# Layer 0's attention scores: one block-diagonal product over 128 rows, or four 32-row tiles of the TensorE array

## The reference

```python
q = hidden_state @ Wq + bq                      # 4096 x 1024 by 1024 x 1024
k = encoder_hidden_state @ Wk + bk              # 256 x 1024 by 1024 x 256
v = encoder_hidden_state @ Wv + bv
scores = jnp.einsum('bkgld,bksd->bkgls', q, k) * scale     # d = 32, s = 64
scores = scores + encoder_attention_mask[:, :, None, :, :]
attn = jax.nn.softmax(scores, axis=-1)
out = jnp.einsum('bkgls,bksd->bkgld', attn, v)
out = out.transpose(0, 3, 1, 2, 4).reshape(b, l, H) @ Wo + bo
x = out + hidden_state                          # then a layer norm
```

## Time and profile before

| | before |
|---|---|
| median of 3 runs | 1936.01 us (1934.52 to 1938.28) |
| the profiled execution, its own time | 1932.28 us |
| its span in the trace | 1930.5 us |
| PE busy, share of the span | 1826.7 us, 95% |
| DVE busy | 1082.6 us, 56% |
| POOL busy | 1032.3 us, 53% |
| ACT busy | 585.9 us, 30% |
| matmuls | 8640 |

### The profile page before, as it was taken

How to read it: one execution, slowest core, us unless ns; L and a number is a source line. 1 busy time by engine, 2 the same in 40 slices (tenths; PEclk the granted TensorE clock), 3 DMA queues, 4 the chain that set the end, 5 groups by cost and what they waited for, 6 DMA issues and landing times.

```text
span 1930.5 us, 22356 instructions
## 1 busy us (share of the span) xinstructions
PE 1826.7 (95%) x8640; PEld 1509.4 (78%) x8640; DVE 1082.6 (56%) x1086; ACT 585.9 (30%) x680; POOL 1032.3 (53%) x580
## 2 busy tenths in 40 slices
PE   5999999999988899999999977999999999999998
PEld 5788888888876777888778856887788778877887
DVE  6888888888867444444344456335633563356342
ACT  3444444444434332233332323112211221122111
POOL 2677777777758755465544656225522552255221
PEclk9999999999999999999999989999999999999999
DMA  8423333233163475655756554422342234132110
GB/s 204 108 76 82 83 79 78 74 81 85 45 191 111 131 235 201 198 180 175 242 188 211 189 189 153 152 77 83 136 153 66 100 118 153 66 118 101 66 55 33
DMA packets 249961, 244.43 MB, mean 127 GB/s; under 512 B 61440, under 2 KB 204928, under 8 KB 249856
## 3 DMA queue, kind: packets, MB, share of 16 engines
q1 hardware_dynamic: 248704, 241.97, 39.9%
q10 hardware_dynamic: 1152, 1.05, 0.2%
HBM read 157.99 MB, written 84.93 MB: 126 GB/s over the span
## 4 chain that ended last, share of the span: by engine, by line
PE 56%; DVE 19%; issue 9%; ACT 6%; POOL 4%; DMA 3%; SPq 2%; ACTq 0%; DVEq 0%; POOLq 0%
PE ps L53 18%; PE ps L55 18%; PE ps L54 18%; DVE small L972 4%; DVE pr L995 3%; ACT pr L741 3%; DVE pT1r L1006 2%; DVE pT0r L1006 2%; PE ps L648 2%; ACT ot L735 2%; DVE xT0r L902 1%; DVE xT1r L902 1%; POOL prob L1280 1%; DVE x2r L1075 1%; DMA xb<-in_x_dram 1%
## 5 line engine op out<-in xcount | busy, mean ns | idle before, releaser
L1275 POOL TENSOR_TENSOR prob<-prob,small 128x1024 f32<-128x1024 f32 x32 | 61.0, 1908 | 397.0 <-DVE small L1086 397.0
L1206 POOL TENSOR_TENSOR pr<-pr,small 128x1024 f32<-128x1024 f32 x64 | 122.0, 1906 | 100.0 <-DVE small L1001 100.0
L1082 DVE SCALAR_TENSOR_TENSOR prob<-ps,bias 128x1024 f32<-128x1024 f32 x32 | 39.1, 1222 | 227.6 <-PE ps L55 227.6
L840 ACT CAST x2Th<-x2r 128x1024 fp32r<-128x1024 f32 x32 | 33.6, 1050 | 424.6 <-DVE x2r L1075 424.6
L1227 POOL TENSOR_TENSOR xb<-xb,bo 128x1024 f32<-128x1024 f32 x32 | 79.9, 2497 | 141.0 <-DMA xb<-in_x_dram 141.0
L1201 POOL TENSOR_TENSOR pr<-pr,small 128x1024 f32<-128x1024 f32 x64 | 124.0, 1938 | 34.8 <-DVE small L976 34.6
L1050 DVE TENSOR_TENSOR y<-ps,xb 128x512 f32<-128x512 f32 x64 | 44.0, 687 | 159.3 <-PE ps L55 156.4
L972 DVE TENSOR_REDUCE small<-pr 128x16 f32<-128x1024 f32 x64 | 78.1, 1220 | 91.0 <-ACT pr L741 91.0
L53 PE MATMUL ps<-wo0h,oc0l 128*128 128x512 f32 x256 | 101.6, 397 | 0.0
L53 PE MATMUL ps<-wo0h,oc1l 128*128 128x512 f32 x256 | 101.0, 395 | 0.0
L53 PE MATMUL ps<-xT0h,wq0l 128*128 128x512 f32 x256 | 100.7, 393 | 0.0
(11 more groups left out here) (320 smaller groups left out, 5583.1 us busy)
## 6 DMA issues: line engine op xcount, KB each, us to landing
o_scratch<-ot SPq DMA_DIRECT2D x256, 64.0 KB, 1.8
ocr<-o_scratch SPq DMA_DIRECT2D x16, 1024.0 KB, 6.2
xb<-in_x_dram SPq DMA_DIRECT2D x32, 512.0 KB, 6.0
x_scratch<-y SPq DMA_DIRECT2D x32, 512.0 KB, 3.5
a_scratch<-ost SPq DMA_DIRECT2D x64, 256.0 KB, 3.0
b_scratch<-ost SPq DMA_DIRECT2D x64, 256.0 KB, 2.5
xd<-x_scratch SPq DMA_DIRECT2D x128, 128.0 KB, 2.8
raw<-b_scratch SPq DMA_DIRECT2D x32, 512.0 KB, 8.0
```

Source lines behind the costliest of these rows:

```text
L1206: nc.gpsimd.tensor_tensor(heads(v), heads(v), mx.unsqueeze(2).to_broadcast([P, TPB * GRP, KEYS]), ALU.subtract)\
L1275: nc.gpsimd.tensor_tensor(prob[:], prob[:], mx1.unsqueeze(2).to_broadcast([P, H1, KEYS]), ALU.subtract)\
```

## The change

The scores are done head by head. A matmul takes 32 of the 128 partitions: the weights are the 32 query rows of one head for one token tile (32 x 128), the moving side is that head's 32 x 64 keys. Four such matmuls, for the four heads, stand one behind the other and write to four different PSUM banks (the view `SJ`: bank = head; a half of each bank for even units and a half for odd ones). With four token tiles and three terms these are 48 matmuls of 64 columns a unit in place of 12 of 256. Since both halves of a bank hold scores, of neighbouring units, the wait before them asks for one unit more: that VectorE has read the scores of unit `v - 1`. VectorE's mask addition reads the new layout. The zeros in `kb` are still written at the start, and no longer read.

```diff
         C2 = ps[:, 0:2048]
+        SJ = ps[:, 1024:3072].rearrange("p (j v m s) -> p v m j s", j=GRP, v=2, m=TPB)
         O, TT = Q, S[0]
@@
                     pe.wait_ge(q_lo, v + 1)
                     pe.wait_ge(k_ld[v % 2], 16 * GRP * (v // 2 + 1))
-                    after(pe, s_read, v - 1)
+                    after(pe, s_read, v)
                     for m in range(TPB):
-                        last = three(nc, S[v % 2][:, 256 * m:256 * (m + 1)], [qs[v % 2][x][:, m] for x in (0, 1)],
-                                     [kb[v % 2][:, :, x] for x in (0, 1)], True, True)
+                        for i, (x, z) in enumerate(((1, 0), (0, 1), (0, 0))):
+                            for j in range(GRP):
+                                head = slice(HD0 * j, HD0 * (j + 1))
+                                last = nc.tensor.matmul(SJ[:, v % 2, m, j], qs[v % 2][x][head, m], kb[v % 2][head, j, z],
+                                                        start=i == 0, stop=i == 2)
                     last.then_inc(scores, 1)
@@
                     nc.vector.tensor_tensor(p[:].rearrange("p j m s -> p m j s"),
-                                            S[v % 2].rearrange("p (m j s) -> p m j s", m=TPB, j=GRP),
+                                            SJ[:, v % 2],
                                             mask[t % 2][:].unsqueeze(2).to_broadcast([P, TPB, GRP, KEYS]), ALU.add)\
```

## The result

The changed kernel takes 1938.97 us (median of 20 runs, 1934.59 to 1945.84) against 1934.76 us before (20 runs): a ratio of 1.0025, 95% interval 1.0015 to 1.0035, some 5 us slower. The forecast was 1980 us. Its range and sign hold, but the size, +44 us, is nine times too large. The range holds only because it was stretched down to the flat rival, whose mechanism is the one that came.

The account below looks back on a forecast made before the run. A DVE and ACT loop was taken as the bound, PE close behind. Added times of 35, 3 and 6 us made 44 us on the profiled 1932.3, so 1976, or 1980 us against the median; range 1934 to 2203 us.

Parts of the forecast that it names:

- the flat rival: Four score tiles run side by side, each set waiting for its loads: 1955 us, or 1936 with free changes; chance 0.24.
- What bounds the kernel: Layer 0's periodic stretch: a DVE and ACT loop paces at 17.10 us a pair; PE has 0.58 us to spare.
- Part 1: PE, scores: the 12 full-array matmuls removed took 1.43 us a unit, 0.119 us each.
- Part 2: PE, scores: the 48 new matmuls are handed over one by one at 39 ns, 1.87 us a unit.
- e: Extra PE time per unit for the scores, forecast as 1.01 us: 2.44 us in place of 1.43.
- Part 3: PE, going over to tiles and back: 0.28 us a time, 0.57 us a unit.
- Part 4: PE's new wait for the previous unit's mask addition costs nothing, since the older wait for `q_lo` implies it.
- Part 5: DVE's mask addition reading the new layout from four banks costs nothing, with 3 us as the bound.
- The sum: Layer 0's total: 35 us periodic stretch, 3 us where PE sets the pace, 6 us at the ends; 44 us more.
- the formula's first term: Periodic stretch: 24.5 pairs, each paying added PE time beyond 0.58 us of slack, 24.5 x (2.02 - 0.58) = 35 us.
- Serial loads: Rival: all 48 score weight loads pass one after another at 107 to 119 ns; 2170 to 2206 us; chance 0.28.
- my own case: Score matmuls handed over at 35 to 80 ns each, +33 to +155 us; likeliest 1980 us; chance 0.40.

Follow-up runs that it names:

- The move of the copy: Kernel before with ScalarE's copy of the value product placed behind the exponential: 1919.23 us, ratio 0.9909; same change in the changed kernel: 1932.32 us, 0.9984.
- the doubled matmuls: Kernel before with the first token tile's three score matmuls done twice: 1938.50 us, ratio 1.0014; with all 12 done twice: 2000.87 us, 1.0345.
- the split: Both kernels with copy behind exponential, scores halved around two query steps: tiled 1951.77 us, ratio 1.0093; full-array 1917.28 us, 0.9927.

## Why the prediction was wrong, point by point

- **What bounds the kernel: right.** A loop of DVE and ACT at 17.1 us a pair, PE 0.58 us behind it. The move of the copy showed the loop, the doubled matmuls the slack.
- **Part 1, the matmuls that go: right,** 1.43 us.
- **Part 2, the matmuls that come: this is the step that failed.** I took 48 x 39 ns = 1.87 us, "handed over one behind the other". Measured: 12 sets at 0.112 us, 1.34 us, on average 28 ns a matmul but in bunches of four. This is 0.53 of the 0.75 us by which e was too large; Part 3 is the rest. The four row groups work side by side, loads and matmuls, and what I called the need of "no assumption that matmuls run beside each other" was itself the wrong assumption. The rule of the Trainium skill that I had beside a rival ("TensorE: Matmul & The Clock Gate", Measured speedup vs the span model: row tiles start some 4 ns apart) agrees with the trace, about 10 ns for the four starts of a set.
- **Part 3, going over and back: right in kind, too dear.** 0.57 us a unit taken, 0.29 measured by the split, 0.32 added up from the starts. A load in the open was there on the way back; the 0.28 us that I took for each way came on neither. The Trainium skill's rule that changing the tiling mode drains TensorE ("TensorEngine Tiling (Array Packing)", Key Properties) agrees with the trace in this: the border costs 0.29 us with tiles, and the same halves on the full array 0.02. Whether the 0.29 us are such a drain no run here shows.
- **Part 4, the wait: no cost was found. Part 5, DVE's reading: right,** L999 takes 1.172 us on average in the periodic stretch, as L995 did.
- **The sum.** With e = 0.26 a pair needs 0.52 us more, less than the 0.58 of slack, and the formula's first term is nothing where I had 35 us. Its rest, 3 x 0.26 and half of 12 x 0.26, gives 2 us; measured are 4 to 5. Between the profiles the parts of layer 0 differ by +1.3 us over the periodic stretch (17.11 to 17.16 a pair), +0.6 behind it and +3 at the two ends; with one profile of each, these parts can't be told from noise. The error in e of 0.75 us, counted over 58 units, makes the error of some 40 us; and e came to lie under the edge of the slack, 0.29 us a unit, where it costs next to nothing.
- **A term that the sum doesn't have: the clock outside the periodic stretch.** The 20 runs of the changed kernel have a mean granted clock of 0.9775, those of the kernel before that were run beside the experiments 0.9816 (56 runs). Within either kernel a run whose clock is 0.001 lower is 0.5 to 0.6 us longer. By that scatter the difference of 0.004 would be some 2 us of the 5, an estimate; whether the lower clock makes the time longer, or both come from longer waits, no run here separates.
- **The rivals.** What came is the second, four tiles side by side and sets at the old pace, which had chance 0.24 with 1936 to 1955 us for free and for dear borders. Serial loads (0.28) and my own case (0.40) are both refuted by the start times. That the sign of the forecast holds is luck as far as Part 2 goes: the sets take 0.09 us less than the matmuls they replace, and only the borders make the unit longer.

## What to carry to other kernels

Row tiles with their own weights run wholly side by side here: a set of four takes 0.112 us, about one weight load, with 64 moving columns and with 128. But where a block-diagonal operand already makes four heads one full-array matmul of 256 columns, that one costs hardly more (0.119 us), so the tiles had little to win (0.09 us a unit), and each excursion to them costs 0.29 us. And before an engine's work is made shorter or longer, its slack against the loop that sets the pace is the first number to find: 0.26 us a unit came with 5 us here, 14 us with the loop shortened; and moving one copy of 0.58 us off that loop was worth 16 us, more than any change here that keeps all the products.

## What the runs showed of the hardware that was not expected

- Row groups are not held to the program's order among each other. With three matmuls in a row on the same 32 rows, the other groups' matmuls from further down the program started in between, and the time stayed the same (1.0027 against 1.0025). The trace speaks here against a sentence of the Trainium skill, "TensorE: Matmul & The Clock Gate", The mechanism, that matmuls start and end strictly in program order. It speaks of the starts alone, since the ends it shows are modelled.
- VectorE's transposition of x (L902, in the changed kernel L906) takes between 2.04 and 2.14 us on average in the periodic stretch, from profile to profile, with tiles and without: 2.06 in the kernel before and 2.12 in the changed one, but 2.13 in the kernel before with the copy moved and 2.05 in the tiled one with it. It stands once a pair on the loop, so the 0.05 us by which the changed kernel's pair is longer can lie in it, and need not be the tiles' doing. What makes the difference stays open.
